# An attention and mixture-of-experts kernel: the first input load, the warm-up products, the last routing and the last routed product are placed elsewhere

## The reference, cut to what matters

```python
x = L0_attn_x                                   # 16 x 256 x 128 = 4096 tokens
x = _layernorm(x + _L0_attn_ref(x, ...))        # causal linear attention, 16 heads of 8
x = _layernorm(x + _L0_ffn_ref(x, ...))         # shared expert + 8 of 32 routed experts
...
q = jnp.exp(q); k = jnp.exp(k)
kv = jnp.cumsum(k[..., None] * v[:, :, None, :], axis=1)
out = einsum(q, kv) / sum(q * cumsum(k))        # then @ Wo.T + bo
...
scores = sigmoid(x @ gate_w.T); choice = scores + gate_bias
# the best 2 of 4 groups by the sum of their 2 best, then the best 8 experts
# weights = scores of the chosen / their sum * 2.5
outs = silu(x @ wg.T) * (x @ wu.T) @ wd.T       # of every expert, 64 wide
final = sum over experts of outs * weight, + shared expert of width 128
```

## Time and profile before

| | |
|---|---|
| median of 3 runs | 458.29 us (457.49 to 458.95) |
| the profiled execution | 457.99 us |
| its span, first to last instruction | 456.2 us |
| busy: PE, DVE, ACT, POOL | 425.7 (93%), 345.7 (76%), 275.8 (60%), 290.6 (64%) us |
| 512-column products of PE | 9 groups of 136, 394 to 456 ns mean |
| POOL product with the routing weight | 128 of 1391 ns mean |
| chain that ended last: PE, DVE, issue, POOL, ACT, DMA | 31, 29, 13, 11, 5, 2% |

### The profile page before, as it was taken

One profiled execution on the slowest core, in us unless ns is written; L12 is line 12 of the kernel. 1 busy time (PEld: TensorE's weight loads), 2 busy tenths in 40 slices (PEclk: granted clock), 3 DMA queues, 4 the chain that ended last, 5 costly groups with the idle time before them and its releaser, 6 DMA issues.

```text
span 456.2 us, 10923 instructions
## 1 busy us (share of the span) xinstructions
PE 425.7 (93%) x4004; PEld 327.3 (72%) x4004; DVE 345.7 (76%) x912; ACT 275.8 (60%) x536; POOL 290.6 (64%) x217
## 2 busy tenths in 40 slices
PE   5888999999999999999999999999999999798992
PEld 3656787768776887868777787868877787476771
DVE  2648777896979877896968967796968968767653
ACT  3746357763696448763696448863697347445642
POOL 2555368745797368754797377755687467666781
PEclk9999999999999999999999999999999999999997
DMA  7500664145454453245463453245452443348300
GB/s 238 210 1 7 174 129 88 34 94 132 96 124 91 102 117 96 49 94 118 93 138 84 100 128 85 57 99 116 93 139 51 104 102 86 61 100 183 94 24 23
DMA packets 28677, 45.10 MB, mean 99 GB/s; under 512 B 2000, under 2 KB 10320, under 8 KB 28240
## 3 DMA queue, kind: packets, MB, share of 16 engines
q1 hardware_dynamic: 28624, 44.40, 40.9%
HBM read 41.77 MB, written 2.62 MB: 97 GB/s over the span
## 4 chain that ended last, share of the span: by engine, by line
PE 31%; DVE 29%; issue 13%; POOL 11%; ACT 5%; DMA 2%; DVEq 1%; ACTq 0%; SPq 0%; POOLq 0%
PE bank L345 30%; DVE units L955 7%; POOL units L1057 6%; DVE stats L801 2%; DVE hidden_lo L781 2%; DVE top_of_group L842 2%; POOL rstd L1076 2%; DVE bank L835 2%; POOL xT_lo L1083 2%; DVE x L813 2%; DMA weight_wide<-weight_d 1%; ACT v_pair L718 1%; ACT hidden_hi L637 1%; DVE replaced L874 1%; DVE out_sb L967 1%
## 5 line engine op out<-in xcount | busy, mean ns | idle before, releaser
L1057 POOL TENSOR_TENSOR units<-units,weight_wide 128x512 f32<-128x512 f32 x128 | 177.4, 1391 | 115.6 <-DVE units L955 106.7
L656 ACT ACTIVATE units<-bank 128x512 f32<-128x512 f32 x136 | 80.7, 594 | 74.0 <-PE bank L345 73.8
L781 DVE TENSOR_TENSOR hidden_lo<-units,hidden_hi 128x512 fp32r<-128x512 f32 x112 | 99.7, 892 | 23.3 <-ACT hidden_hi L637 23.3
L637 ACT ACTIVATE hidden_hi<-units 128x512 fp32r<-128x512 f32 x136 | 86.0, 633 | 51.1 <-POOL units L1057 49.4
L955 DVE TENSOR_TENSOR units<-bank,units 128x512 f32<-128x512 f32 x136 | 93.1, 685 | 29.8 <-PE bank L345 22.7
L345 PE MATMUL bank<-x_hi,gate_hi 128*128 128x512 f32 x136 | 62.1, 456 | 5.1 <-DVE units L955 4.8
L345 PE MATMUL bank<-x_hi,up_hi 128*128 128x512 f32 x136 | 54.5, 401 | 2.9 <-ACT units L656 2.9
L345 PE MATMUL bank<-hidden_hi,down_hi 128*128 128x512 f32 x136 | 54.9, 404 | 2.5 <-DVE hidden_lo L781 1.3
L345 PE MATMUL bank<-x_lo,gate_hi 128*128 128x512 f32 x136 | 54.1, 397 | 0.0
L345 PE MATMUL bank<-x_hi,gate_lo 128*128 128x512 f32 x136 | 53.9, 396 | 0.0
L345 PE MATMUL bank<-x_hi,up_lo 128*128 128x512 f32 x136 | 53.9, 396 | 0.0
(11 more groups left out here) (125 smaller groups left out, 689.2 us busy)
## 6 DMA issues: line engine op xcount, KB each, us to landing
weight_wide<-weight_d SPq DMA_DIRECT2D x62, 512.0 KB, 6.6
xT<-xT_in SPq DMA_DIRECT2D x8, 256.0 KB, 6.7
x_tok<-x_in SPq DMA_DIRECT2D x8, 256.0 KB, 7.0
out_dram<-out_sb SPq DMA_DIRECT2D x7, 256.0 KB, 2.3
weight_wide<-up_in SPq DMA_DIRECT2D x1, 1088.0 KB, 8.5
up_raw<-up_in SPq DMA_DIRECT2D x1, 1088.0 KB, 10.6
down_raw<-down_in SPq DMA_DIRECT2D x1, 1088.0 KB, 12.8
weight_d<-weightT SPq DMA_DIRECT2D x8, 64.0 KB, 1.6
```

The costliest lines, as they stand in the source:

```text
L637: nc.scalar.activation(hidden_hi[place(n, g)][:, :], units[place(n, g)][:, :], ACT.Copy).then_inc(hidden_hi_done, 1)
L656: nc.scalar.activation(units[place(n, g)][:, :], up_banks[2 * n % 3][:, :], ACT.Silu).then_inc(silu_done, 1)
L781: V.tensor_tensor(hidden_lo[place(n, g)][:, :], units[place(n, g)][:, :], hidden_hi[place(n, g)][:, :].bitcast(F32), ALU.subtract).then_in ...
L1057: G.tensor_tensor(units[place(n, g)][:, :], units[place(n, g)][:, :], weight_wide[:, w % (2 * PIECE), :], ALU.mult).then_inc(hidden_done, 1)
```

## The change

It has these parts.

- ScalarE's queue issues the first load of xT; SP no longer does.
- VectorE first sets `neg_half` and a new 384-column tensor `unread`; PE multiplies it by itself four times (256 columns) into a bank nobody reads, before it waits for the attention weights. The product of `bv_wide` with `woT` and its addition to `row_bias` come later, behind the projections and the scans of the first group.
- The down weights are requested after the rows of group 1 and after the up weights' arrival.
- The scan of the second group (`k_totals(1)`) stands behind the first `normalise` on VectorE, not among the units products.
- The last routing (`m = 7`): x1's transposes are in slot 8 (`turned_at`) instead of 9, the gate product in 9, the exponentials' transpose in 10; `group_tops`, `masked_experts`, the choice (split off as `chosen_experts`) and `expert_weights` take slots 11 to 14, and the weights' transpose slot 15 (`weights_at`). The second piece of the last weights is requested right behind the first.
- The product of the last routed block with its weight is VectorE's instead of GpSimd's.

```diff
+        unread = sb("unread", [128, 384])
...
+        def turned_at(m):
+            return 9 if m < GROUPS - 1 else 8
+        def weights_at(m):
+            return 14 if m < GROUPS - 1 else 15
@@ sync
-                if front and n == 5:
+                if front and f > 0 and n == 5:
...
                 if front and f > 0 and n == 12:
                     load_rows(f)
+                    if f == 1:
+                        sp.wait_ge(up_loaded, 16)
+                        sp.sem_inc(apart, 1)
+                        sp.dma_start(down_raw, down_d).then_inc(down_loaded, 16)
...
-                    sp.dma_start(down_raw, down_d).then_inc(down_loaded, 16)
...
                         load_wide(0, m, 1 - u)
+                    if m == GROUPS - 1:
+                        load_wide(1, m, 1 - u)
-                if ffn and n == 2:
+                if ffn and n == 2 and g < GROUPS - 1:
                     load_wide(1, g, u)
...
-                sp.wait_ge(hidden_done, reached(ROUTED * g + (1 if p == 1 else PIECE * (p - 1))))
+                sp.wait_ge(hidden_done, reached(ROUTED * g + (1 if p == 1 and g < GROUPS - 1 else PIECE * (p - 1))))
@@ tensor
+            pe.wait_ge(setup_chain, 2)
+            for _ in range(4):
+                mm(y_bank[:, 0:256], unread[:, 0:128], unread[:, 128:384])
             pe.wait_ge(w_attn_loaded, 32)
-            pe.wait_ge(setup_chain, 1)
-            mm(mid_banks[0][:, 0:DIM], bv_wide[:, :], woT).then_inc(bias_mm, 1)
...
-                if mid and n == 10:
+                if mid and n == turned_at(m) + 1:
...
-                if mid and not front and n == (10 if m == 0 else 11):
+                if mid and not front and n == 10:
                     turn_exponentials(m)
...
-                if mid and n == 9:
+                if mid and n == turned_at(m):
...
+                if g == -2 and n == 11:
+                    pe.wait_ge(setup_chain, 3)
+                    mm(mid_banks[0][:, 0:DIM], bv_wide[:, :], woT).then_inc(bias_mm, 1)
...
-                if mid and n == 14:
+                if mid and n == weights_at(m):
@@ scalar (its n == 9, 10, 14 of mid change in the same way)
+            nc.scalar.dma_start(xT[:, :], xT_d[:, 0:GROUP]).then_inc(xT_loaded, 16)
+            act.wait_ge(setup_chain, 1)
+            nc.scalar.activation(rstd1[:, :], neg_half[:, :], ACT.Exp)
             act.wait_ge(w_attn_loaded, 32)
-            act.wait_ge(setup_chain, 2)
-            nc.scalar.activation(rstd1[:, :], neg_half[:, :], ACT.Exp)
...
                     act.wait_ge(gated_done, reached(BLOCKS * g + n + 1))
+                elif g == GROUPS - 1 and block_at(n, g) == ROUTED:
+                    act.wait_ge(last_hidden_done, 1)
@@ vector
+            V.memset(neg_half[:, :], -0.5).then_inc(setup_chain, 1)
+            V.memset(unread[:, :], 0.0).then_inc(setup_chain, 1)
             dve.wait_ge(w_attn_loaded, 32)
...
+                if g == GROUPS - 1 and block_at(n, g) == ROUTED:
+                    dve.wait_ge(wide_loaded[PIECES - 1], loads_of(PIECES - 1, GROUPS))
+                    dve.wait_ge(gated_done, BLOCKS * g + n + 1)
+                    V.tensor_tensor(units[place(n, g)][:, :], units[place(n, g)][:, :],
+                                    weight_wide[:, 2 * PIECE - 1, :], ALU.mult).then_inc(last_hidden_done, 1)
...
                     normalise(x1[1 - u], resid, mean_var, rstd1, x1_done)
+                    if m == 0:
+                        k_totals(1)
...
-                if m == 0 and mid and n == 14:
-                    k_totals(1)
...
                 if mid and n == 10:
                     expert_scores(m)
+                if mid and n == (10 if m < GROUPS - 1 else 11):
                     group_tops(m)
-                if mid and n == 11:
+                if mid and n == (11 if m < GROUPS - 1 else 12):
                     masked_experts(m)
-                if mid and n == 12:
+                if mid and n == (12 if m < GROUPS - 1 else 13):
+                    chosen_experts(m)
+                if mid and n == (12 if m < GROUPS - 1 else 14):
                     expert_weights(m)
@@ gpsimd
-                if ffn and block_at(n, g) > 0:
+                if ffn and block_at(n, g) > 0 and (g < GROUPS - 1 or block_at(n, g) < ROUTED):
...
-                if mid and n == 9:
+                if mid and n == turned_at(m):
```

More of the change, by code:

```diff
@@ L187, in attention_moe_kernel @@
         out_done, out_stored, last_done = (sem(n) for n in ("out_done", "out_stored", "last_done"))
+        last_hidden_done = sem("last_hidden_done")
         wide_loaded = [sem(f"wide_loaded{p}") for p in range(PIECES)]
@@ L767, in _, with rows_bias @@
             V = nc.vector
+            V.memset(neg_half[:, :], -0.5).then_inc(setup_chain, 1)
+            V.memset(unread[:, :], 0.0).then_inc(setup_chain, 1)
             dve.wait_ge(w_attn_loaded, 32)
             V.tensor_copy(bv_wide[:, :], attn_cols[:, 2:3].to_broadcast([128, 128])).then_inc(setup_chain, 1)
-            V.memset(neg_half[:, :], -0.5).then_inc(setup_chain, 1)
             dve.sem_inc(resid2_done, 1)
-            dve.wait_ge(const_loaded, 48)
-            dve.wait_ge(bias_mm, 1)
-            V.tensor_tensor(row_bias[:, :], mid_banks[0][:, 0:DIM], row_bias[:, :], ALU.add
-                            ).then_inc(bias_done, 1)
+            def rows_bias():
+                dve.wait_ge(const_loaded, 48)
+                dve.wait_ge(bias_mm, 1)
+                V.tensor_tensor(row_bias[:, :], mid_banks[0][:, 0:DIM], row_bias[:, :], ALU.add
+                                ).then_inc(bias_done, 1)
             def low_part(n, g):
@@ L865, in masked_experts, with chosen_experts @@
                     float(TOP_GROUPS), by_group(choice[:, :]), ALU.is_lt, ALU.mult), m, 9)
-            def expert_weights(m):
+            def chosen_experts(m):
                 for i in range(TILES):
@@ L876, in expert_weights @@
                 linked(last, m, 11)
+            def expert_weights(m):
                 dve.wait_ge(weight_turned, reached(m))
@@ L999, in slot @@
                 if front and f == 0 and n == 14:
+                    rows_bias()
                     dve.wait_ge(q_exp, 1)
```

## The result

| | before | after |
|---|---|---|
| median | 458.12 us (457.49 to 458.95, 6 runs) | 460.92 us (460.12 to 461.62, 6 runs) |
| the profiled execution, its span | 457.99, 456.2 us | 461.33, 459.5 us |
| mean granted clock of PE | 0.994 | 0.987 |

The changed kernel is slower: ratio 1.0059, 95% interval 1.0043 to 1.0075, or 2.8 us. I had forecast 458.7, no change that can be told. The range, 456.2 to 461.0, held the time with only 0.08 us to spare; the likeliest case did not come.

The account below looks back on a forecast made before the run. PE's order was taken to bound the six middle groups, which the change leaves alone. Terms -2.2 - 0.45 + 3.75 - 0.65 = +0.45 gave 458.7 us on the median's scale, range 456.2 to 461.0.

Parts of the forecast that it names:

- the likeliest case: Whole kernel: gains at the ends are given back in the last routing; 457.2 to 459.9 us, chance 0.45.
- The start: First 50 us: earlier PE work brings the faster pace sooner, so masked queries end earlier; -2.2 us, ends -0.9 and -2.7.
- both near 4.5: Start: xT and the attention weights compete as loads and both land near 4.5 us, so projections start at 4.65, 0.7 gained.
- The second scan: First groups: moving VectorE's scan frees GpSimd's k_sum product and shortens hidden_lo; -0.45 us, ends -0.65 and 0.
- The last routing: Last group: late silu (1.93 us) and three more VectorE pieces (1.83) make weights 3.75 us later; ends +0.7 and +4.2.
- So the lateness passes on whole, +3.75.: After the last routing: the wait for weights through memory is a chain, so all 3.75 us reach the end.
- The second piece: Last weights: requesting both pieces together removes a GpSimd wait of 2.16 us that was hidden; 0, or 0.9 if uncovered.
- rival C: Last weights: two pieces share the engines, stretching the first by up to 3.8 us; middle +1.9, 460.6 us, chance 0.12.
- first weights more than 7 us after their issue: Last weights: the landing time that would show the two pieces sharing the engines, rival C.
- The last product: Kernel's end: moving GpSimd's product to VectorE lets PE start at 445.65 instead of 446.29; -0.65 us, ends -0.75 and 0.
- Tables: ScalarE in the last routing: each table load costs 1.28 us without a drain; with the skill's drain, 2.76 us worse.
- A: Whole kernel, as summed: gains at the ends, given back in the last routing; 457.2 to 459.9 us, chance 0.45.

Follow-up runs that it names:

- late_piece: The changed kernel with the second piece of the last weights requested after the first product, as before the change: 459.02 us, ratio 1.0025 to the kernel before.
- warm_late: late_piece with eight unread 256-column products on PE where it waits for the last group's weights: 459.00 us, ratio 1.0019 to the kernel before.
- warm_wait: The changed kernel with eight unread 256-column products on PE where it waits for the last group's weights: 459.72 us, ratio 1.0045 to the kernel before.

## Why the prediction was only partly right

- **The start** (-2.2, ends -0.9 and -2.7). Alone it gave -2.72, at the lower end. The pace changed earlier, as forecast, but three steps of the working failed. The landing "both near 4.5" holds for the weights, but PE also needs the attention columns, and they came at 4.9 to 5.5. VectorE's maskings were to end at about 10.5; they took 2.95 us, ended at 12.56, and the scores waited for them, so that the scores of the changed kernel gained 0.77 us and not 2.2. Another 0.93 came behind them, nearly all from PE's stop of 1.34 us among the products with `probs`, which the working did not have; why it is there and goes is not shown. In the profiled execution of the changed kernel the gain up to the first transposes of x1 was 1.7, in that of the start alone 2.0. That the term came out near -2.2 is in part luck. What I credited to x's earlier request cannot be told from nothing (0.9923 without it, 0.9916 with it), and 1.18 of the 2.72 came without the unread products.
- **The second scan** (-0.45). 0.53 in the trace, 0.92 in the medians: right in kind, a little small.
- **The last routing** (+3.75). 3.76 from transposes to transposes. The steps of its working are all in the rows: the silu of slot 10, then units, then scores; three pieces more of the feed-forward work. It was the largest term, and an order followed on paper gave it to 0.01 us (part of that is luck), in its halves 1.85 and 1.85.
- **"So the lateness passes on whole, +3.75."** This step failed, by being too small. On medians the whole routing, without the early request, costs 5.0 us (459.02 against 454.04). The trace of the late piece shows 3.76 up to the weights' transposes and 0.46 from there to GpSimd's product, because the first piece lands later, and nothing more; the rest of the 5.0 is open. I also treated the wait as an empty gap of PE that has no cost of its own. Alone that was right (late_piece, warm_late); with the early request on top, PE's idle time went from 0.45 to 3.85 us, its products ran slow for 6 us, and that cost 1.28 us, which the unread products bought back (warm_wait).
- **The second piece** (0). This failed most. The wait that it removes was indeed hidden, but the request made the first piece later: 7.93 against 7.20 with the late request, and the landing is on the path. It cost about 1.7 us on medians; the traces have 0.73 for the landing and the 1.28 for the longer fall of the clock that follows from it. It is near rival C, to which I gave 0.12 at 1.9 us. Its sign, "first weights more than 7 us after their issue", was a poor one, for the late request meets it too. Its working failed in that the second request joined 2.4 us behind the first and not 1.1, since it waits for GpSimd, and in that one part of 32 was stretched and not all of them. I weighed against it that three loads at the start landed in the order of their issue. Landing in order does not say that the first is not held up. The Trainium skill, in "DMA: Bandwidth & Descriptors", Queues, rings and completion order, has each DMA engine alternate between the queue rows that have work. I concluded that two requests on one row do not share: 31 parts of 32 bear that out, the last does not (later by 0.7 and 1.2 us than with the late request). For two rows the start agrees (attn_w 2.7 to 3.8 us).
- **The last product** (-0.65). -0.36 on medians, -0.46 and -0.41 in traces: I charged three low parts behind it and got two waits in place of one.
- **Tables.** The load back stood from 385.16 to 386.44 and the silu followed at 386.45: no drain beyond the load, against what the Trainium skill, in "ScalarE: Activation LUTs", What ACT_TABLE_LOAD costs, adds.

In sum, against a forecast of +0.45 and a result of +2.80: gains at the ends 0.54 larger (3.84 for 3.3), the routing 1.23 dearer (4.98 for 3.75), and the early request 1.66 instead of 0. That a later landing makes PE's wait longer, and the longer wait costs its clock, was in none of my rivals, and C and A were priced as if they excluded one another. Without the early request the sum would have missed by 0.7 us (459.02 against 458.3 on that set's scale).

What stays open: whether the instruction load is what delays the first piece in the five-slot kernels (7.20 to 7.40 us with the late request, against 6.71 to 7.00 in the others), and why a second request makes the one late part later still; and why the medians of the five-slot kernels lie above their profiled executions (459.02 and 458.43, 457.76 and 456.9). With the late piece, the seven executions with a mean granted clock under 0.99 took 459.4 us on average and the five others 458.7. But with PE kept busy in its wait the median is the same (459.00) and the spread no smaller, and with the five slots alone the clock does not part the long executions from the short. So the clock explains little of it, as far as these runs show.

## What to carry to other kernels

A routing chain that ends in a round trip through memory is on the path from its first instruction: moving one link earlier helps only if every engine it passes has nothing late in its queue ahead of it. Follow each engine's order by hand; that gave the size here. When a wait of PE grows from half a microsecond to several, allow for the price of its clock (0 to 1.3 us here), and when a request moves nearer to one that somebody waits for, allow for a later landing (0.1 to 1.8 us here); then ask whether the two feed each other. The best version keeps the start, the scan and the last product and leaves the routing and its second piece alone: 454.04 us, 0.8% under the kernel before.

## What the runs showed of the hardware

- After 3.1 us of idle time PE was granted 1.2 GHz until 416 us, and after 3.85 us until 420, though its mean clock over the span only went from 0.994 to 0.992 and 0.987. After 3.33 us, in another kernel's trace, it kept 2.4 GHz. With eight unread products of 256 columns in the gap it was kept in both kernels that had them.
- A piece of 1024 KB on one queue lands 6.71 to 7.00 us behind the chain's previous step, and 7.20 to 7.40 where a 16 KB instruction load falls among its data; then one part of 32 is late. With a second piece requested 2.4 us behind it as well: 7.93 and 8.51. With a second piece 4.6 us behind it and no instruction load among its data: 6.83.
- At the start the page grants full clock throughout, while a 512-column pass takes 1093 ns on average in one execution and 900 ns in another. The column is no guide in the first 10 us; the durations are.
